# Edge counts of a two-layer graph kernel: one gathered tile of 128 edge slots for each pair of nodes

## What is computed

```python
def layer0(x):                                   # D_FF = 286, types of 2
    n = ln_weight * x * rsqrt(mean(x * x) + 1e-6)
    out = n @ W_root + bias
    for r in range(2):
        w = edge_type_2 == r
        sums = segment_sum((n[src] @ W_rel[r]) * w, dst)
        out += sums / maximum(segment_sum(w, dst), 1)
    return x + elu(out) @ wo
x = layernorm(x + layer0(x))                     # so y = elu(..) @ wo is added to 2 x
u = x @ root + bias + sum over 8 types of (mean of x[src] over edges of the type) @ weight[r]
z = concat([u, x]) @ w_gate + b_gate
x = layernorm(x + tanh(u) * z + x * (1 - z))
```

## Time and profile before

| | |
|---|---|
| time, median of 3 runs | 943.87 us (943.1 to 945.9) |
| profiled execution, span | 943.8 us; no time of it outside the span is given |
| first instructions to the first product at full pace | 0 to 70.42 us |
| loop of windows and first product | 70.42 to 163.98 us |
| rest of first layer, second layer, gate, output | 163.98 to 943.8 us |
| PE busy | 884.8 us (94%) |
| DVE busy | 734.1 us (78%) |
| ACT busy | 463.5 us (49%) |

### The profile page before, as it was taken

One profiled execution on the slowest core, in us unless ns is written; L12 is line 12 of the kernel. 1 busy time (PEld: TensorE's weight loads), 2 busy tenths in 40 slices (PEclk: granted clock), 3 DMA queues, 4 the chain that ended last, 5 costly groups with the idle time before them and its releaser, 6 DMA issues.

```text
span 943.8 us, 18917 instructions
## 1 busy us (share of the span) xinstructions
PE 884.8 (94%) x7117; PEld 646.1 (68%) x7118; DVE 734.1 (78%) x1206; ACT 463.5 (49%) x752; POOL 18.2 (2%) x44
## 2 busy tenths in 40 slices
PE   3659999899998999999999999999999999999996
PEld 2537787645467776776786786687687687678542
DVE  5779998595998777777777777777877877776777
ACT  5754445445565545535535535535544453553811
POOL 1000001000000000000000000000000000000000
PEclk9879999899999999999999999999999999999998
DMA  8101000251202222022022022022112202302302
GB/s 264 40 2 51 1 0 1 98 217 68 90 1 90 90 90 89 2 91 90 0 89 89 0 89 89 12 77 89 47 41 89 84 5 90 112 2 90 112 23 87
DMA packets 30375, 63.43 MB, mean 67 GB/s; under 512 B 1513, under 2 KB 4721, under 8 KB 30321
## 3 DMA queue, kind: packets, MB, share of 16 engines
q1 hardware_dynamic: 30321, 62.71, 18.8%
HBM read 57.52 MB, written 5.18 MB: 66 GB/s over the span
## 4 chain that ended last, share of the span: by engine, by line
PE 78%; DVE 13%; issue 4%; ACT 4%; DVEq 1%; POOL 0%; POOLq 0%; ACTq 0%
PE psP L1055 41%; PE psA L1125 18%; PE psP L853 6%; PE psP L904 5%; PE psA L893 4%; DVE wsplit L1311 2%; PE psP L980 1%; DVE wsplit L1305 1%; PE psA L842 1%; DVE stats L1508 1%; DVE u_mem L1553 1%; DVE p_mem L1355 1%; DVE wsplit L1428 1%; ACT u_mem L614 1%; ACT wsplit L553 1%
## 5 line engine op out<-in xcount | busy, mean ns | idle before, releaser
L1055 PE MATMUL psP<-wsplit,xT 128*128 128x256 f16 x2592 | 296.4, 273 | 3.2 <-ACT vec L741 2.8
L1055 PEld LDWEIGHTS psP<-wsplit,xT 128*128 128x128 f16 x2592 | 254.3, 98 | 37.5 <-issue 3.1
L1125 PE MATMUL psA<-p_mem,c_mem 128*128 128x512 f16 x800 | 175.3, 379 | 0.0
L1055 PE MATMUL psP<-wsplit,x 128*128 128x256 f16 x1296 | 150.3, 273 | 1.7 <-DVE key_mem L1619 1.5
L1125 PEld LDWEIGHTS psA<-p_mem,c_mem 128*128 (+1 forms) x800 | 78.2, 98 | 91.0
L1055 PEld LDWEIGHTS psP<-wsplit,x 128*128 128x128 f16 x1296 | 126.7, 98 | 16.8 <-issue 2.2
L1311 DVE SCALAR_TENSOR_TENSOR wsplit<-stage,sc,wsplit 128x1024 f16<-128x1024 f32 x90 | 114.7, 1278 | 27.1 <-ACT wsplit L564 27.1
L564 ACT ACTIVATE wsplit<-stage,sc 128x1024 f16<-128x1024 f32 x90 | 100.6, 1137 | 15.0 <-DVE sc L1202 9.1
L853 PE MATMUL psP<-p_mem 125*128 125x140 f16 x1125 | 77.7, 231 | 18.0 <-ACT u_mem L578 12.9
L853 PEld LDWEIGHTS psP<-p_mem 125*128 125x128 f16 x1125 | 74.8, 101 | 22.4 <-ACT u_mem L578 8.3
L1584 DVE SCALAR_TENSOR_TENSOR u_mem<-psA,coef,u_mem 128x512 f32<-128x512 f32 x80 | 60.0, 750 | 33.0 <-PE psA L1125 30.9
(11 more groups left out here) (199 smaller groups left out, 802.8 us busy)
## 6 DMA issues: line engine op xcount, KB each, us to landing
stage<-in_L_gnn_weight SPq DMA_DIRECT2D x16, 2048.0 KB, 8.0
stage<-in_L_gnn_w_gate SPq DMA_DIRECT2D x4, 2048.0 KB, 7.9
x_home<-x SPq DMA_DIRECT2D x5, 512.0 KB, 2.6
x<-x_home SPq DMA_DIRECT2D x5, 512.0 KB, 5.5
stage<-in_L_gnn_W_rel SPq DMA_DIRECT2D x4, 572.0 KB, 7.6
x<-in_x SPq DMA_DIRECT2D x1, 2048.0 KB
xT<-in_L_gnn_root SPq DMA_DIRECT2D x1, 2048.0 KB, 9.9
stage<-in_L_gnn_root SPq DMA_DIRECT2D x1, 2048.0 KB, 8.2
```

Of the source, the lines that this page charges most:

```text
L1055: last = nc.tensor.matmul(psP[:, bank, (col + tt) * FB:(col + tt + 1) * FB], lhs[tt](a, c), split_block(n, b)[:, c, :], start=(first and t ...
L1125: last = nc.tensor.matmul(psA[:, (NT * h + t) % 2, :], cnt8[:, r, s, t * P:(t + 1) * P], p_part[h][a][:, s, :], start=(s == 0 and a == 0), ...
```

## The change

1. The edges are laid out anew: partition p holds 160 consecutive edges and 96 more of the following partition (`RUN`, `SPAN`), by eight transfers, four of them issued by ACT. From the target numbers DVE works out, for each of 320 pairs of nodes and each of five starting points in a run (steps of 32), whether the pair's edges begin there (`starts`, 0 or 1).
2. PE gathers with these as a selection matrix (`gather`, 27 matmuls of 320 columns): for each pair of nodes a column of 128 edge slots with three numbers each: `LOW`, which lies below 128, and two keys (target, source tile and type), one for the types of 8 and one for the types of 2. DVE and ACT copy them to SBUF, each number repeated 8 or 10 times (`lo_spread`, `key_spread`).
3. Ten pairs make a batch (32 batches). DVE makes the one-hot tiles of a batch by two `tensor_tensor` comparisons, all operands 16-bit (1280 and 1000 elements per partition). PE does one matmul for each pair, 128 slots x 128 low numbers times 128 slots x 100 columns (5 source tiles x 2 nodes x 10 types). ACT copies two banks of 500 columns for each batch.
4. x is loaded, squared, rooted and normed by tiles; the norming moves from ACT to DVE; x is no longer doubled, instead `cy` is halved and the first layer norm uses a quarter of its epsilon.
5. ACT's square-root table and POOL's all-reduce are each used once on a spare value near the start.
6. The table of windows and the second form are gone; a check that every pair fits (`order_checks`) feeds a flag, and a general form runs after the loop if the flag is set. For the given inputs the largest pair has 82 edges and the flag is 0.

In item 2 the source number is split in a part below 128 and the tile: `LOW` is `src` minus 16 times a masked number, and the masked number is what the keys carry. The diff, cut to its core:

```diff
@@ sizes @@
-WIN = 14
-NWIN = -(-NODES // WIN)
-WCOLS = WIN * (R0 + R1)
-MEET = 5
+RUN = 160
+STEP = 32
+SPAN = RUN + P - STEP
+PAIR = 2
+NWIN = NPAD // PAIR
+PCOLS = PAIR * REL_ALL
+BANK_WINS = 5
+BATCH = 2 * BANK_WINS
+NB = NWIN // BATCH
+SUB = 8
+EARLY = 4 * BATCH
+AHEAD = NB - 4 * NT
@@ SP @@
-            sp.dma_start(x[:, 0:NT - 1, :], x_d[0:(NT - 1) * P, :].rearrange("(t p) d -> p t d", p=P)).then_inc(x_loaded, 16)
+            for t in range(2, NT - 1):
+                sp.dma_start(x[:, t, :], x_d[t * P:(t + 1) * P, :]).then_inc(x_loaded[t], 16)
...
@@ POOL, after the iotas @@
+            pool.wait_ge(seed_ready, 4)
+            nc.gpsimd.partition_all_reduce(spare[:, :], eps[:, 3:4], P, RMAX).then_inc(consts_ready, 1)
@@ ACT @@
+            def square_x(t):
+                act.wait_ge(x_loaded[t], 16 if t < NT - 1 else 32)
                 nc.scalar.activation(xs[:, t, :], x[:, t, :], ACT.Square, accum_out=ss[:, t:t + 1]).then_inc(sumsq_ready, 1)
...
+            def copy_bank(m, bank, copied):
+                src = psP[:, bank, 0:BANK_COLS].rearrange("p (s n r) -> p r s n", s=NT, n=BANK_NODES)
+                nc.scalar.activation(cnt[:, :, :, bass.ts(m, BANK_NODES)], src, ACT.Copy).then_inc(copied, 1)
...
+            square_x(0)
+            square_x(1)
+            spread_keys(0, EARLY)
+            square_x(2)
             split_hi(0, 0, xT, X_GAIN)
+            spread_keys(EARLY, NWIN)
+            square_x(3)
             split_hi(0, 1, xT, X_GAIN)
+            copy_batches(0, 1)
+            square_x(4)
             split_hi(0, 2, xT, X_GAIN)
+            copy_batches(1, 2)
             split_hi(0, 3, xT, X_GAIN)
+            copy_batches(2, 3)
             split_hi(0, 4, xT, X_GAIN)
+            copy_batches(3, 4)
             w0_sum(0)
+            copy_batches(4, 8)
             w0_sum(1)
+            copy_batches(8, 10)
             act.wait_ge(w0_scaled, 1)
             w0_high(0)
+            copy_batches(10, AHEAD)
             w0_high(1)
@@ PE @@
+            def gather(out, *parts):
+                terms = [(fields[:, a, k * STEP:k * STEP + P], starts[:, k, :]) for a in parts for k in range(KT)]
...
+            def count_batch(k, b):
+                pe.wait_ge(onehot_ready, k + 1)
+                for i in range(2):
+                    pe.wait_ge(win_copied, 2 * k + (i + 1))
+                    out = psP[:, 2 * b + i, 0:BANK_COLS].rearrange("p (s n r) -> p s (n r)", s=NT, n=BANK_NODES)
+                    for j in range(BANK_WINS):
+                        jj = i * BANK_WINS + j
+                        last = nc.tensor.matmul(out[:, :, j * PCOLS:(j + 1) * PCOLS], oh_lo[:, b, jj, :],
+                                                oh_key[:, b, jj, :].rearrange("p (s w) -> p s w", s=NT),
+                                                start=(j == 0), stop=False, skip_group_check=True)
+                    last.then_inc(win_counted, 1)
@@ DVE @@
+            for k in range(KT + 1):
+                last = ts(below[:, k, :], win_row[0:EP, :], firsts[:, k:k + 1], None, ALU.is_gt)
+            step(last)
+            tt(starts, below[:, 0:KT, :], below[:, 1:KT + 1, :], ALU.subtract).then_inc(starts_ready, 1)
+            step(ts(hi_int, src, 4, 8 * (NT + 2), ALU.logical_shift_right, ALU.bitwise_and))
+            stt(fields[:, LOW, :], hi_int, -16.0, src, ALU.mult, ALU.add).then_inc(fields_ready, 1)
...
+            def norm_x(t):
+                dve.wait_ge(rms_std_ready, t + 1)
+                step(nc.vector.reciprocal(rstd[:, 0, t:t + 1], std[:, 0, t:t + 1]))
+                ts(xs[:, t, :], x[:, t, :], rstd[:, 0, t:t + 1], None, ALU.mult).then_inc(xs_ready, 1)
...
+            def onehot_batch(k, b):
+                dve.wait_ge(win_counted, 2 * k + 2)
+                low = lo_spread[:, bass.ts(k, BATCH), :].unsqueeze(2).broadcast_to([P, BATCH, P // SUB, SUB])
+                key = key_spread[:, bass.ts(k, BATCH), :].unsqueeze(2).broadcast_to([P, BATCH, NT * PAIR, REL_ALL])
+                tt(oh_lo[:, b, :, :].rearrange("p j (a b) -> p j a b", b=SUB), low_table, low, ALU.is_equal)
+                tt(oh_key[:, b, :, :].rearrange("p j (a r) -> p j a r", r=REL_ALL), key_table, key,
+                   ALU.is_equal).then_inc(onehot_ready, 1)
...
+            norm_x(0)
+            norm_x(1)
+            spread_low(0, EARLY, 1)
+            dve.wait_ge(consts_ready, 7)
+            dve.wait_ge(keys_spread, 2)
+            onehot_batches(0, 1)
+            norm_x(2)
+            split_x_lo(0)
+            onehot_batches(1, 2)
+            spread_low(EARLY, NWIN, 2)
+            norm_x(3)
+            split_x_lo(1)
+            onehot_batches(2, 3)
+            norm_x(4)
+            split_x_lo(2)
+            onehot_batches(3, 4)
...
-            onehot_windows(6, AHEAD)
+            onehot_batches(6, AHEAD)
...
-            onehot_windows(AHEAD, FIRST - 1)
+            onehot_batches(AHEAD, FIRST - 1)
...
-            onehot_windows(FIRST - 1, FIRST)
+            onehot_batches(FIRST - 1, FIRST)
...
+            with dve.If(wrong_order >= 1):
+                onehot_any()
```

More of the change, by code:

```diff
@@ L159, in build @@
+        LOW, DST64, KEY8, KEY2 = range(4)
         st_mem = stage[:, :, :].rearrange("p s w -> p (s w)")
@@ L352, in scale_col, with block_batch, by_twos @@
             return i if i <= U_WO else 2 + slot
[L354 to L365, removed]
+        def block_batch(t, n):
+            return 4 * t + (AHEAD + n)
+        def by_twos(engine, k0, k1, batch):
+            if k1 - k0 > 3:
+                with engine.Fori(0, (k1 - k0) // 2) as it:
                     for b in range(2):
[L367 to L370, removed]
+                        batch(2 * it + (k0 + b), (k0 + b) % 2)
+                k0 = k1 - (k1 - k0) % 2
+            for k in range(k0, k1):
+                batch(k, k % 2)
         GATE = [(0, 0), (1, 0), (0, 1), (1, 1)] + [(t, h) for t in range(2, NT) for h in range(2)]
@@ L844, in turn @@
                     last.then_inc(turned, 1)
-            pe.wait_ge(table_ready, 1)
-            most_chunks = pe.value_load(most[0:1, 0:1], min_val=1, max_val=CH)
-            def count_chunk(b, src, win, first):
-                for s in range(NT):
-                    col = (s % 3) * WCOLS
-                    last = nc.tensor.matmul(psP[:, 2 * b + s // 3, col:col + WCOLS], src[:, s * P:(s + 1) * P], win,
-                                            start=(first and s % 3 == 0), stop=False, skip_group_check=True)
-                return last
@@ new lines, in count_batches, with count_any, quad @@
+            def count_batches(k0, k1):
+                by_twos(pe, k0, k1, count_batch)
+            def count_any():
+                def quad(bank, q, first):
+                    pe.wait_ge(any_ready, q + 1)
+                    slot = q % ANY_RING
+                    for e in range(ANY):
+                        last = nc.tensor.matmul(psP[:, bank, 0:BANK_COLS], ring_lo[:, slot, e, :], ring_key[:, slot, e, :],
+                                                start=(first and e == 0), stop=False, skip_group_check=True)
+                    last.then_inc(any_used, 1)
+                with pe.Fori(0, BANKS // 2) as it:
+                    for b in range(2):
+                        q0 = (2 * it + b) * (RUN // ANY)
+                        pe.wait_ge(any_copied, 2 * it + (b + 1))
+                        quad(b, q0, True)
+                        with pe.Fori(1, RUN // ANY) as p:
+                            quad(b, q0 + p, False)
```

549 lines of the change are left out of this document (244 added, 305 removed).

## The result

The changed kernel takes 897.1 us (median of 4 runs, 896.8 to 897.2), the kernel before 944.0 (4 runs, 943.1 to 945.9): ratio 0.9495, 95% interval 0.948 to 0.951. The forecast was 894 with a range of 883 to 914. The profiled execution took 897.08 us, with a span of 895.0; so 2.1 us lie outside its span. Against the span of before, 943.8, the span is 48.8 us shorter; the sum of the prediction, made on spans, was 49.5. The medians differ by 46.9 us only. In the other runs of the kernel before, 1.8 to 2.4 us lie outside the span, so its profiled execution was one of some 945.9 us, the slowest of the four, and about 1.9 of the 48.8 us is spread between its executions; where in the span they lie the trace doesn't say. For the same reason the forecast's 894.3 is a span, to be held against 895.0. The total fits better than its parts do.

What follows compares the result with a forecast made beforehand. PE was taken to bound the count loop, with DVE close behind and late ahead of it. From the 943.8 us span, 42.8 (loop) and 6.7 (earlier start) come off: 894.3, say 894; range 883 to 914.

Steps and rivals of the forecast that it cites:

- The loop: Count loop: 19 products and 18 batches plus waits take 50.8 us, 42.8 less than 93.56.
- the wait behind each half product: In the loop, PE waits about 0.1 us per half tile for one-hots; a half tile given 5.4 us, not 5.28.
- The chain: In the loop, product end through ACT's high part and DVE's two instructions to the next one-hots: 2.7 us against 2.64.
- DVE's rate: DVE's two 16-bit comparisons do two elements a cycle, 1.45 us a batch.
- one step to it: For DVE's comparisons, 32-bit times of 1225 and 814 ns taken to mean one tensor does twice as many elements as two.
- Edges at 6.5 us: At the start, four more transfers issued by ACT, x just behind them: edges in at 6.5 us, before 4.41.
- ACT late ahead of the loop: Ahead of the loop, ACT's work from 16 us sets the last W0 sum at 48.5 us; DVE has some 30 us.
- rival (b): Ahead of the loop, waits between engines are 10 to 15 us, not 2.5; loop starts at 71 to 78; chance 20%.
- The first all-reduce: Ahead of the loop, POOL's 6.2 us before its all-reduce is a first-use price, paid early on a spare value.
- After the loop: equal: Behind the loop, the new jump over the general form costs what the old 3.15 us did; bounds 3 less, 2 more.

Runs made afterwards that it cites:

- experiment on single elements: The changed kernel, but a batch's first comparison reads one low number 8 times with step 0 instead of a row of 8 equal numbers; 910.3 us, ratio 0.9642.

## Why the prediction was right, point by point

- **The loop** (42.8 us less, measured 40.8). Count matmuls of 44 ns, blocks of 2.64 us and ACT's copies (L612, 598 ns for 500 elements) came out as worked out. The term that was too small is the wait behind each half product: I gave 0.12 us a half tile, and the 3.1 us that the loop lost to it are 0.34. The chain was the right one, but it is longer than I had it. A block takes 2.64 us without a wait; behind a first half it takes 2.95, behind a later one 3.1. For the later half the chain takes 77.67 to 80.55 = 2.9 us, not 2.7: ACT's high part has 429 columns there and takes 0.53 us, where I had the 0.29 of a first half's 143, and 0.28 us lie between ACT's end and DVE's start. And I counted from the modelled end of the product (72.77), while PE is at its next matmul 0.16 us before (72.61).
- **DVE's rate** (1.45 us a batch, measured 1.33). Two elements a cycle, taken between rows of one and of four, was right, though one step to it was loose: 1225 and 814 ns are as 1.5 to 1, not 2 to 1. The experiment on single elements shows by what: for the first comparison, only because each number is written out 8 times.
- **Edges at 6.5 us** was wrong: 15.95. I had put x "just behind them" as if one queue were in order with the other. SP's x transfers were asked for between ACT's edge transfers, and the small rows came through last. That moved the keys by 9.7 us, from 16 to 25.7.
- **ACT late ahead of the loop** was right in its sum and not in its reason. From the keys to the last sum I had 32.5 us and it took 30.5; from the scale to the loop 13.4 where it took 12.1. But DVE is as busy there as ACT, 27.97 of 30.50 us against 28.10, and the chain of waits between them has 16.0 us of DVE, 6.2 of ACT and 4.7 of PE. Its longest pieces:

```profile
31.31 2.41 DVE wsplit L1266
52.27 3.96 ACT cu_mem L644 x8
```

  It runs on DVE for the most part to 46.5 us, and ends with ACT's sums. The slower comparison agrees: 14 batches of 0.67 us more are 9.3, and the loop started 7.1 us later. "ACT, not DVE, is late" doesn't hold. With the late edges these terms give a start at 70.0 for 63.7: 6.3 us late, just short of rival (b)'s 71 to 78, and by the edges, not by engines waiting for each other as (b) had it.
- **The first all-reduce** (6.2 us given back) was right, its use worth 5.3 us in time.
- **After the loop: equal** was wrong: 7.6 us less. I priced the jump by its row, 3.15 us, and took the new program to pay the same, with 3 us as the bound. Left out were the 1.41 us ahead of it in the same gap and the low clock behind it, and the new program has no gap there: 6.1 us. The other 1.5 us are the clock at the start of the second layer.

So an overestimate of the gain by 6.3 + 2.0 us ahead of and in the loop met an underestimate by 7.6 behind it. The forecast's 894 owes its closeness to that, which is luck, and 1.5 us of it is the luck of a clock.

## What to carry to other kernels

A broadcast operand of a two-tensor 16-bit instruction is worth writing out into short rows: with eight copies the comparison took 816 ns, with one element read eight times 1481. When a transfer on which the first work hangs is moved or split, look at what large transfer is asked for in the same microseconds on any queue, and hold that one back. And count the code that a kernel jumps over for cases that don't occur: here it cost 6.1 us, a gap and a low clock behind it, which no group of instructions in the profile carries.

## What the runs showed that I had not expected

- Eight small edge transfers (rows of 640 and 384 bytes, 0.5 MB together) land 5.5 us after ACT has asked for the last of them (at about 2.6 us) even with no x beside them, and 13.3 us after it with x beside them.
- PE's clock was at its lower level for 3.3 us behind an idle stretch of 4.76 us, though PE had been busy without a break for 93.56 us before it; and at two places of the later stages it was low in some kernels and whole in others, behind the same instructions and equal waits.
- The time of an execution lies 1.9 to 2.2 us above the span of its profile in each of the profiled runs (897.08 and 895.0, 890.57 and 888.4, 898.09 and 896.2).
